# The third attention of a four-layer kernel: stacks of queries and keys fetched through scratch memory, first maxima in row tiles, the quotient in two instructions

## What is computed

```
xn = layernorm(x)
q1, q2 = xn @ q1_w.T, xn @ q2_w.T          # 16 heads of 8
k1, v  = context @ kv1_w.T;  k2 = context @ kv2_w.T (keys)
a1 = softmax(q1 k1^T / sqrt(8)) v
a2 = softmax(q2 k2^T / sqrt(8)) v
a  = lambda_1 * a1 - lambda_2 * a2         # per head, up to sign in the code
x  = x + rms_norm(a) @ proj_w.T + proj_b
```

## Time and profile before

| | |
|---|---|
| median of three runs | 1170.75 us (1169.52 to 1181.66) |
| the profiled execution's own time | 1185.0 us |
| its span, first to last instruction | 1183.0 us, mean granted clock 0.879 |
| the third attention, first to last products and sums | 533.5 to 709.3 us of the span |

### The profile page before, as it was taken

How to read it: one execution, slowest core, us unless ns; L and a number is a source line. 1 busy time by engine, 2 the same in 40 slices (tenths; PEclk the granted TensorE clock), 3 DMA queues, 4 the chain that set the end, 5 groups by cost and what they waited for, 6 DMA issues and landing times. The chain is left out here.

```text
span 1183.0 us, 18800 instructions
## 1 busy us (share of the span) xinstructions
PE 958.5 (81%) x6856; PEld 767.3 (65%) x6856; DVE 573.2 (48%) x1602; ACT 512.1 (43%) x947; POOL 395.0 (33%) x372
## 2 busy tenths in 40 slices
PE   4888999999988999848788794689557886299982
PEld 3566899999977989724344333589534654188882
DVE  7875411211275333642544636245298785444443
ACT  2665634444355434412333430465345552155552
POOL 4544210000042103400000054355646557645552
PEclk9999999999998999965777975699869997599997
DMA  9999900000000000022222110566310001345543
GB/s 351 189 184 192 197 1 2 1 1 1 1 2 1 1 1 1 22 70 69 59 53 63 29 32 30 181 198 217 89 40 1 1 1 37 121 157 178 168 151 107
DMA packets 80490, 94.63 MB, mean 80 GB/s; under 512 B 8721, under 2 KB 64120, under 8 KB 80272
## 3 DMA queue, kind: packets, MB, share of 16 engines
q1 hardware_dynamic: 74256, 82.90, 29.1%
q0 software_dynamic: 4992, 8.45, 2.1%
q10 hardware_dynamic: 1152, 2.10, 0.5%
HBM read 52.34 MB, written 32.18 MB: 71 GB/s over the span
## 5 line engine op out<-in xcount | busy, mean ns | idle before, releaser
L2778 ACT ACTIVATE hT<-PS,par 128x512 f32<-128x512 f32 x200 | 136.4, 688 | 174.6 <-PE PS L2682 173.1
L2818 DVE SCALAR_TENSOR_TENSOR X<-PS,wts,X 128x128 f32<-128x128 f32 x272 | 76.5, 344 | 218.7 <-PE PS L2701 218.6
L2701 PEld LDWEIGHTS PS<-regA,hT 128*128 128x128 f32 x1024 | 119.1, 192 | 3.1 <-issue 0.5
L2701 PE MATMUL PS<-regA,hT 128*128 128x128 f32 x1024 | 119.5, 275 | 0.0
L1590 POOL TENSOR_TENSOR score<-score,mx 128x1232 f32<-128x1232 f32 x32 | 72.0, 2249 | 90.0 <-DVE mx L1461 90.0
L2449 PE MATMUL PS<-q_up,halves 128*112 128x256 f32 (+1 forms) x276 | 85.3, 309 | 9.2 <-DVE hT L2558 9.1
L1088 DVE TENSOR_REDUCE score<-PS 128x8 f32<-128x616 f32 x64 | 49.6, 796 | 79.0 <-PE PS L979 78.7
L2680 PE MATMUL PS<-x_up,w_halves 128*128 128x512 f32 x200 | 87.1, 435 | 0.1
L2681 PE MATMUL PS<-x_low,w_halves 128*128 128x512 f32 x200 | 80.1, 400 | 0.0
L2450 PE MATMUL PS<-q_up,halves 128*112 128x256 f32 (+1 forms) x276 | 79.3, 287 | 0.0
L2682 PE MATMUL PS<-x_up,w_halves 128*128 128x512 f32 x200 | 79.3, 396 | 0.0
(11 more groups left out here) (355 smaller groups left out, 2081.9 us busy)
## 6 DMA issues: line engine op xcount, KB each, us to landing
regA<-L3f_w SPq DMA_DIRECT2D x23, 704.0 KB, 4.1
regB<-L2f_w SPq DMA_DIRECT2D x23, 578.0 KB, 3.8
L2f_sorted_x<-empty_row SPq DMA_DIRECT2D x8, 1161.0 KB, 20.4
L3f_sorted_x<-empty_row SPq DMA_DIRECT2D x8, 1161.0 KB, 19.5
regA<-L0f_w SPq DMA_DIRECT2D x4, 768.0 KB, 16.3
regA<-L2f_sorted_x SPq DMA_DIRECT2D x23, 129.0 KB, 3.6
regB<-L3f_sorted_x SPq DMA_DIRECT2D x23, 129.0 KB, 4.0
par<-params SPq DMA_DIRECT2D x1, 2637.0 KB, 13.1
```

The lines of the kernel that those rows point to most:

```text
L2701: last = nc.tensor.matmul(PS[:, 4 + n % 2, j * P:j * P + P], hT[0:rows, n % 2, k, j * P:j * P + P], w2[0:rows, e, k, :], start=k == 0, sto ...
L2778: nc.scalar.activation(hT[:, n % 2, k, :], PS[:, i % 4, :], c["act"], bias=pc(f"{tag}_b1")[:, col:col + 1]).then_inc(h_ready.sem, 1)
L2818: nc.vector.scalar_tensor_tensor(X[:, t, :], PS[:, 4 + n % 2, j * P:j * P + P], wts[:, t, e:e + 1], X[:, t, :], ALU.mult, ALU.add)\
```

## The change

The stacks are laid out anew, so that a key stack is one tile with all four row groups beside one another, and so are two of the query stacks; the third is in two pieces (one row group, three row groups). Two scratch tensors are added. All keys are stored to one of them by two copies, the queries of each sequence and set to the other by two copies of 128 partitions. `keys(i)` is then three copies from scratch, each for all four row groups, `queries(i)` three (six where the stack is in two pieces), after a wait for the store. The ones are one copy.

The maxima of pass 0 are computed straight from the tiles of halves, three 32-row matmuls for each row group. In step 0 of a pass TensorE does the values and sums of the last step between the two halves of the products; in the other steps the order is as before. ScalarE does the reciprocal between the two exponentials of step 0. VectorE divides ahead of maxima 6 and 7, the quotient first and the check second, each with a signal of its own: the values of the next pass wait for the first, its sums for the second. Some signals get names that other stages use as well.

```
+        q_stack_0, q_stack_2b = under("q_stack_a", [4 * 512, 3 * 512], skip=[2 * NT * ROW])
...
-        key_stack_2 = [key_piece_b, key_piece_c] + key_pieces_a
+        key_stack_1, key_stack_2 = under("key_stack_a", [RG * HR * K, RG * HR * K], skip=[2 * B * HR * K])
+        key_stack_0, q_stack_1, q_stack_2a = under("stack_b", [RG * HR * K, 4 * 512, 512], skip=[6 * B * HR * K])
+        key_stacks = [key_stack_0, key_stack_1, key_stack_2]
+        q_parts = [[(0, q_stack_0)], [(0, q_stack_1)], [(0, q_stack_2a), (1, q_stack_2b)]]
+        q_stacks = [[tile[:, 512 * r:512 * r + 512] for _, tile in parts for r in range(tile.shape[1] // 512)] for parts in q_parts]
...
+            def key_stack(i):
+                return key_stacks[i % 3][:, :].rearrange("p (r n) -> p r n", r=RG)
+
+            def moves(i):
+                return 9 if i % 3 == 2 else 6
...
+                def store_keys():
+                    sp.wait_ge(kb_ready.sem, kb_ready.at(4 * sets))
+                    for s in range(sets):
+                        sp.dma_start(keys_dram[s, :, :], kb[:, s, :, :, :, :].rearrange("p u b h k -> p (u b h k)").bitcast(F32)).then_inc(keys_stored.sem, 16)
+
+                def store_queries(b, s):
+                    sp.wait_ge(q_ready.sem, q_ready.at(sets * b + s + 1))
+                    for u, half in enumerate(q[s]):
+                        c = slice(512 * b, 512 * b + 512)
+                        sp.dma_start(q_dram[s, u, :, c], half[:, c].bitcast(F32)).then_inc(q_stored[s][b % 2].sem, 16)
+
+                def free_stack(i):
+                    if i >= 3:
+                        sp.wait_ge(prod_ready.sem, prod_ready.at(6 * (i - 2)))
+
                 def keys(i):
                     b, s = divmod(i, sets)
-                    sp.wait_ge(kb_ready.sem, kb_ready.at(2 * sets if b == 0 else 4 * sets))
-                    if i >= 3:
-                        sp.wait_ge(prod_ready.sem, prod_ready.at(6 * (i - 2)))
+                    free_stack(i)
+                    sp.wait_ge(keys_stored.sem, keys_stored.at(32))
+                    src = keys_dram[s, :, :].rearrange("(r p) (u b n) -> u b p r n", p=32, u=2, b=B)
                     for m, u_k in enumerate((0, 0, 1)):
-                        for r in range(RG):
-                            dims, at = slice(32 * r, 32 * r + 32), slice(32 * m, 32 * m + 32)
-                            sp.dma_start(key_stack(i, r)[at, :].bitcast(F32), kb[dims, s, u_k, b, :, :].rearrange("p h k -> p (h k)").bitcast(F32))\
-                                .then_inc(stack_rows[i % 3].sem, 16)
+                        sp.dma_start(key_stack(i)[32 * m:32 * m + 32, :, :].bitcast(F32), src[u_k, b, :, :, :]).then_inc(stack_rows[i % 3].sem, 16)
 
                 def queries(i):
                     b, s = divmod(i, sets)
-                    up, low = q[s]
-                    sp.wait_ge(q_ready.sem, q_ready.at(sets * b + s + 1))
-                    for m, half in enumerate((up, low, up)):
-                        for r in range(RG):
-                            dims, at = slice(32 * r, 32 * r + 32), slice(32 * m, 32 * m + 32)
-                            sp.dma_start(q_stack(i)[at, r, :].bitcast(F32), half[dims, 512 * b:512 * b + 512].bitcast(F32))\
-                                .then_inc(stack_rows[i % 3].sem, 16)
+                    free_stack(i)
+                    sp.wait_ge(q_stored[s][b % 2].sem, q_stored[s][b % 2].at(32 * (b // 2 + 1)))
+                    for m, u in enumerate((0, 1, 0)):
+                        src = q_dram[s, u, :, 512 * b:512 * b + 512].rearrange("(r p) n -> p r n", p=32)
+                        for r0, tile in q_parts[i % 3]:
+                            dst = tile[32 * m:32 * m + 32, :].rearrange("p (r n) -> p r n", n=512).bitcast(F32)
+                            sp.dma_start(dst, src[:, r0:r0 + tile.shape[1] // 512, :]).then_inc(stack_rows[i % 3].sem, 16)
 
                 def ones(n):
-                    for r in range(RG):
-                        sp.dma_start(key_stack(n, r)[96:96 + 2 * HR, :].bitcast(F32), minus_head[0:2 * HR, :].bitcast(F32)).then_inc(stack_ones[n].sem, 16)
+                    sp.dma_start(key_stack(n)[96:96 + 2 * HR, :, :].bitcast(F32),
+                                 minus_head[0:2 * HR, :].bitcast(F32).unsqueeze(1).to_broadcast([2 * HR, RG, HR * K])).then_inc(stack_ones[n].sem, 16)
 
                 def shift_rows(i):
                     sp.wait_ge(shift_ready.sem, shift_ready.at(i + 1))
                     for r in range(RG):
-                        sp.dma_start(q_stack(i)[96:96 + 2 * HR, r, :].bitcast(F32), shiftT[32 * r:32 * r + 2 * HR, :].bitcast(F32)).then_inc(stack_shift.sem, 16)
+                        sp.dma_start(q_stack(i, r)[96:96 + 2 * HR, :].bitcast(F32), shiftT[32 * r:32 * r + 2 * HR, :].bitcast(F32)).then_inc(stack_shift.sem, 16)
 
                 sp.wait_ge(constants.sem, constants.at(1))
+                ones(0)
+                store_keys()
+                keys(0)
+                for read, n_read in frees:
+                    sp.wait_ge(read.sem, read.at(n_read))
+                store_queries(0, 0)
+                store_queries(0, 1)
+                queries(0)
+                queries(1)
                 ones(1)
-                for (read, n_read), load in zip(frees, (keys, queries)):
-                    sp.wait_ge(read.sem, read.at(n_read))
-                    load(0)
-                ones(0)
                 keys(1)
-                queries(1)
                 ones(2)
+                store_queries(1, 0)
                 shift_rows(0)
+                store_queries(1, 1)
                 for i in range(2, passes + 1):
                     if i < passes:
+                        if i % 2 == 0 and i >= 4:
+                            store_queries(i // 2, 0)
+                            store_queries(i // 2, 1)
...
+                    if i == 0:
+                        pe.wait_ge(kb_ready.sem, kb_ready.at(2 * sets))
+                        for m, (half, u_k) in enumerate(((x_up, 0), (x_up, 1), (x_low, 0))):
+                            for r in (2 * h, 2 * h + 1):
+                                dims = slice(32 * r, 32 * r + 32)
+                                last = nc.tensor.matmul(PS[:, bank + r % 2, 0:HR * K], half[dims, j * P:j * P + P], kb[dims, 0, u_k, 0, :, :],
+                                                        start=m == 0, stop=m == 2)
+                        last.then_inc(max_psum.sem, 1)
+                        return
                     pe.wait_ge(*loaded_rows(i))
                     for r in (2 * h, 2 * h + 1):
...
                         pe.wait_ge(stack_shift.sem, stack_shift.at(16 * RG * (i + 1)))
-                        pe.wait_ge(stack_ones[i % 3].sem, stack_ones[i % 3].at(16 * RG))
+                        pe.wait_ge(stack_ones[i % 3].sem, stack_ones[i % 3].at(16))
+                        pe.wait_ge(*loaded_rows(i))
...
                 def sums(n):
-                    k = n % 3
+                    i, k = divmod(n, 3)
+                    if k == 0 and i:
+                        pe.wait_ge(check_used.sem, check_used.at(i))
...
                     parts = extras(n)
-                    for h in range(2):
-                        if n < steps:
-                            do(("prod", 2 * n + h))
-                        for use in parts[h]:
-                            do(use)
-                    if 0 < n <= steps:
+                    if n < steps:
+                        do(("prod", 2 * n))
+                    for use in parts[0]:
+                        do(use)
+                    if n % 3 == 0 and 0 < n <= steps:
+                        values(n - 1)
+                        sums(n - 1)
+                    if n < steps:
+                        do(("prod", 2 * n + 1))
+                    for use in parts[1]:
+                        do(use)
+                    if n % 3 and n <= steps:
                         values(n - 1)
                     for use in parts[2]:
                         do(use)
-                    if 0 < n <= steps:
+                    if n % 3 and n <= steps:
                         sums(n - 1)
                     for use in parts[3]:
...
                     quotient = (w_first, w_second)[s]
-                    nc.vector.tensor_tensor(w_check, PS[:, 7, :], w_rec, ALU.mult).then_inc(v_step, st.one())
                     if s == 0:
                         ins = nc.vector.tensor_tensor(quotient, PS[:, 6, :], w_rec, ALU.mult)
                     else:
                         ins = nc.vector.scalar_tensor_tensor(quotient, PS[:, 6, :], lam[:, 0:1], w_rec, ALU.mult, ALU.mult)
                     ins.then_inc(sums_used.sem, 1)
-                    v.wait_ge(v_step, st.n)
+                    nc.vector.tensor_tensor(w_check, PS[:, 7, :], w_rec, ALU.mult).then_inc(check_used.sem, 1)
 
...
                         for p in (3, 4, 5):
                             maxima(8 * (i + 1) + p)
```

(35 more changed lines are left out.)

23 lines of the change are left out of this document (8 added, 15 removed).

## The result

The changed kernel takes 1141.24 us (median of 4 runs, 1139.5 to 1142.18), the kernel before beside it 1176.2 us (4 runs, 1169.52 to 1186.32): ratio 0.9694, 95% interval 0.961 to 0.9778. The forecast was 1131, from 1112 to 1154. The profiled execution takes 1140.5 us, its span is 1138.7 us; before it was 1185.0. The forecast for that execution was 1138.

A forecast was written before the change was run, and what follows sets the result against it. TensorE was taken to be held by SyncE's load issues, late division quotients and half clock behind those waits. Head -7 and passes -40 bring 1185.0 us to 1138; the median, between 1138 and 1124, was put at 1131, range 1112 to 1154.

The forecast's parts named there:

- The queue: SyncE's issues in a third-attention pass: 12 to 15 copies instead of 28, 7.8 to 9.8 us instead of 18.2.
- The loads' time: A pass's 1230 KB from scratch memory: 8 us, hidden under 11 us before the rows are read.
- The bound of 3 us each for passes 2 and 4: In these passes four query stores (1 MB, 7 us) precede the loads: up to 3 us longer each.
- The head: Ahead of pass 0's first product: shift ends at 521.5, product at 525.5 instead of 533.5; -7 us, from -4 to -10.
- The 1 us kept back for bank turns: Allowance in the stretch before pass 0's first product for bank turns with VectorE: 1 us, leaving -7 us.
- The pass: One third-attention pass: 14.5 us at full clock, 16 with routing or output projection; eight taken at 17, -40 us.
- The clock: TensorE's clock in the third attention: 128 us at full, 152 at half; 136 taken, passes 1 to 6 above 0.85.
- Rival B: Third attention: TensorE's bank pauses keep most passes at 1.2 GHz; 1154 us for the profiled execution, 1147 median; chance 0.22.
- D: Third attention: VectorE and the shift rows become the wait instead; -12 us, 1159; chance 0.11.
- C: Third attention: loads from scratch memory too slow, 22 us each against 11 of cover; +19, 1190 us; chance 0.05.
- Behind the stage: After the third attention: POOL's 16 scatters end about when the last root's input comes; 0 to +2 us.
- The middle: Median forecast: 1138 if the profiled execution's 14 us over the median were clock lost in this stage, otherwise 1124; 1131 taken.

The follow-up runs named there:

- experiment 1: Changed kernel with its loads put back to 24 tile-to-tile copies of one row group each, without stores to scratch memory: 1159.0 us, +17.
- experiment 2: Changed kernel with its loads still from scratch memory, stores kept, but in 24 copies of one row group each: 1150.7 us, +8.4.
- experiment 6: Changed kernel with each load's rows also copied to an unread second place in scratch memory, 6 more issues a pass: 1148.9 us, +6.6.
- experiment 5: Changed kernel with only pass 0's maxima put back to 96-row products from the stack: 1144.9 us, +2.7.
- experiment 4: Changed kernel with one engine's part of the division put back alone: ScalarE's 1146.8 us, VectorE's 1153.4, TensorE's order 1154.5.

## Why the prediction was right, and where it was off

**The queue.** Forecast 12 to 15 copies and 7.8 to 9.8 us a pass: 14 copies in 7.8 us (pass 4's loads and stores, pass 3's shift rows), and 13 in 6.8 (pass 5's loads, pass 4's shift rows), by 0.43 us for a load and 0.66 for a shift copy. TensorE no longer waits for loads. Experiments 1 and 2 show the cause; that an issue is itself cheaper than the 0.59 to 0.66 of before was left out of the sum, which took today's 0.65 on purpose.

**The loads' time.** 8 us at worst was right (slowest single copy 8.0, one pass's load alone 6). The bound of 3 us each for passes 2 and 4 came to nothing; experiment 6 shows it would not have taken much more. The estimate of at least 5.6 us worked out from the Trainium skill's page "SBUF — State Buffer", "Door 1: The DMA port swizzle", is not contradicted by those 6 us (1230 KB, 205 GB/s on average). Single slices reach 344 GB/s, above the page's 218: three copies into different partitions are in flight at once, and no run here sets one apart.

**The head.** Forecast 525.5 and 521.5 for the shift's end; 525.52 and 521.35 in the trace. That the first product came within 0.02 us is luck: in the second trace of the same kernel it is at 522.85, 43.5 us behind SP's first copy and not 44.6. The row-tile pairs ran from 509.45 to 516.4, 7 us and not 8. The 1 us kept back for bank turns was not needed. The prediction set the ones copies at nothing, "under other waits". The idle queue of the changed kernel bears it out; beside slow loads they are worth 4 us (experiment 5).

**The pass.** At full clock 14.5, or 16 with extras, was forecast: pass 1 is 14.7, passes 3 and 5 are 16.0. Inside, two terms were mis-sized: the wait behind the reciprocal is 1.08 us, not 0.5, and the shift rows are late once, by 0.26 and not 0.5 (the row names no releaser; the last shift copy ends 1.4 us before it), so they are not the largest wait left, which the prediction said would be seen. Missing altogether was the wait for the squares. The prediction had VectorE's order from the code and never followed it beyond the quotient to the square sums. So three of the six passes from 1 to 6 fell outside the 15 to 18 us that were to show the forecast: 20.2, 20.9 and 20.7 (pass 1, 14.7, is just below). The forecast of 17 us a pass, 1 above full clock, came out as 17.3 (138.1 / 8) in part by luck: half clock in passes 0, 2, 4 and 6 made up for passes 1 and 7, shorter than the 16 us of the sum.

**The clock.** 0.90, where "above 0.85" was forecast for passes 1 to 6: 1.00, 0.83, 1.00, 0.84, 1.00, 0.92, so passes 2 and 4 miss it. Pass 0 began at half clock as said (0.63, 16.2 us). Rival B is excluded by these rows, D by the 0.5 us that turn waits for VectorE, C by the absence of waits for loads. Rival B's argument, that short pauses bring the clock down, holds in part: three passes did show it.

**Behind the stage.** +2.2 where 0 to +2 was forecast.

**The median.** The step that missed is the last one of the sum, "The middle: **1131 us**". The profiled execution went 44.5 us down (47 forecast), the median 29.5 from the 1170.75 of the sum (35 from the 1176.2 beside it), where 40 was forecast. The prediction held both readings of the 14 us by which the profiled execution stood above its median, 1138 if they lay in this stage, and took the middle without a row for it. Before and changed kernel differ in their spread also: before ran from 1164.57 to 1188.88 over all runs here, the changed kernel from 1139.5 to 1143.37, and the long runs are those of low clock: 1164.57 us at a mean of 0.899 over the span, 1187.77 at 0.876. That fits a stage that flipped between clock levels from run to run and no longer does, and so the reading of 1138. That this spread lay in this stage was not measured; only one execution of before has a trace.

## What to carry to other kernels

Where a granted clock sags, price a wait at its own length plus the half-clock work behind it: 1.1 us of waiting cost 4 us here, 2.0 cost 4.2. Not every short wait does so; the 1.08 us waits of passes 1, 3 and 5 had full clock behind them. So after a change look for the next short wait, however small it is in the list: it may have been hidden behind the one just removed. A queue of many small copies is a cost per issue: count them all, the small constant ones too, and read their issue time in the trace before thinking of bytes. And take the median's forecast from where the profiled execution stands apart, not from the middle.

## What the runs showed of the hardware beyond that

- Issue time on SP's queue grew little with the size: from scratch memory, 32 rows of 1232 bytes took 0.42 us (experiment 2), 128 such rows in one copy 0.43 to 0.45 (changed kernel, medians). It differs with the kind of copy and with what stands ahead in the queue: tile to tile 0.59 (experiment 1), stores from a tile to scratch memory 0.43 to 0.45, the same loads behind copies within scratch memory 0.59 (experiment 6), where the second piece of a query load, behind the first, takes 0.42. What sets it is open.
- In pass 1 of the changed kernel TensorE stood 1.08 and then 0.36 us within 2 us and kept full clock (1.00); in pass 2 a further 1.08 us, 4 us later, was followed by half clock for some 7 us; 1.98 us after the first pair did the same (experiment 4).
- Key stores of 1232 KB each landed 6.2 to 8.8 us after issue, query stores of 256 KB in 2.6 to 7.5.
